# Sample weights, depthwise sums and a leaky ReLU operand of VectorE in PSUM, and query scaling in four pieces

## The chip, the cores and the metric

The kernel runs on one core of one Trainium2 chip. The metric is the device time of one execution in microseconds (us), lower is better. Its engines are named as the profile names them: PE is TensorE, DVE is VectorE, ACT is ScalarE, POOL is GpSimd, SP is SyncE.

## What is computed

The reference adds four layers to an image x of shape (4, 256, 64, 64), each on the group-normalised x. Cut to what the change touches:

```python
# layer 0: deformable convolution, then a gated MLP
y = leaky_relu(bn1(conv1x1(gn(x))), 0.01)
t = leaky_relu(bn(depthwise3x3(y) + dw_b), 0.01)
offset, mask = linear(t), softmax(linear(t), 9 taps)      # G = 4 groups, 9 taps each
samp = bilinear(inproj(y), grid(offset))                   # 4 corners of each tap are read
dout = outproj((samp * mask).sum(taps))
x2   = bn2(y + dout); x3 = x2 * se(x2.mean())
x    = x + y + fc2(leaky_relu(fc1(x3), 0.01))
# layer 1: 3x3 grouped convolution with rotated kernels, modulated
# layer 2: linear attention: q = softmax(q, over the 64 of a head) / 8, k = softmax(k, over pixels)
#          out = Wout . (context(k, v) . q), then batch norm over all images
# layer 3: three grouped convolutions with 4-bit weights
```

## The kernel before, in words

The work is written as programs of the five engines that wait on each other by semaphores. A list called `plan` runs stages for each of the 4 images (b = 0 to 3): A (convolution, depthwise convolution, offsets and masks), F (outproj and MLP), L1, L2, and last L3 for all images. Inside, stage A has loops A1 and A2, F has F1 and F2, L2 has L2a and L2b. Each loop has four turns of two chunks of 512 pixels.

The sampling runs beside these stages, as a stream. POOL does nothing else: for each image it walks over 32 tiles of 128 pixels, and in each over 4 groups. For one tile and one group (a **unit**) it issues 9 indirect DMAs, called gathers here, from the table in HBM into the group's slot of `ring` (L371). So the stream has 4 x 128 = 512 units and 4608 gathers. The slot's semaphore `ring_free` holds POOL back until DVE has used what lies in the slot; with four slots POOL can be four units ahead.

The DVE part of a unit is `unit` in the vector program. It waits for the gathers, multiplies the slot's 2304 numbers a partition with 36 sample weights, each broadcast over 64 channels, in `PARTS` = 4 instructions of 576 numbers (L1340), and sums them with one reduction (L1346). Both `ring` and the weights `wt` are in SBUF. `Stream.give` puts these units between the DVE instructions of the stages. `TURNS` says how many tiles a turn of a stage takes; `extra` puts single tiles (one of 4 units) between stages. That gives these numbers of tiles, over all images:

| where | tiles | units |
|---|---|---|
| A1 / A2 | 12 / 12 | 48 / 48 |
| extra tiles in A, in L1 | 8, 3 | 32, 12 |
| F1 (with the last one) / F2 | 16 / 24 | 64 / 96 |
| L1 / L2a / L2b | 20 / 24 / 9 | 80 / 96 / 36 |

Image 0 passes stage A before the stream begins, and image 3 passes F2, L1, L2 and then L3 runs after it has ended.

Other names that the change touches:

- A2: `depthwise` makes half of the depthwise convolution on DVE: for each of 9 taps and two chunks one instruction on 512 numbers, a product first (L1484), then product and sum (L1486), from `padded` in `img2` into `dwacc`, a piece of `img1` in SBUF. ACT reads `dwacc` and writes `ych`. The other half is on PE, in banks 0 and 2 of the PSUM tensor `PS`.
- F2: for each chunk four quarters q of the hidden layer. PE fills two banks (`up`, semaphore gH), ACT adds the bias into SBUF (gZ), DVE makes the leaky ReLU of 1024 numbers with `leaky` (L1405, both inputs are the same SBUF tile; gB), and PE multiplies the result (`down`, gD). `room(pe, "gZ", ...)` lets PE write a bank again.
- L2a: for each chunk DVE scales `QS`, the exponentials of 512 pixels' queries, 2048 numbers a partition, with the reciprocals `qsum` (L1775), for PE to transpose (cQn).
- `PS` has 8 banks of 512 numbers. A1, F1, F2 and L2a use banks 6 and 7 for their matmuls.

Of the kernel before, what the change touches and what calls it, by code (L numbers as in the profile page):

```python
# [20 lines left out]
ALU = mybir.AluOpType  # L21
# [111 lines left out]
def network_kernel(nc, x, par, wa, wr, wf, wq, w3, out):  # L133
    ctx = ExitStack()
    with ctx:
# [36 lines left out]
        ostats = sb("ostats", [P, KC * B * CHUNKS * 6])  # L172
        sm = sb("sm", [P, 496])
        PS = ctx.enter_context(nc.psum_tensor("PS", [P, 8, 512], F32))

        def v(name, k=None, rows=P):
# [16 lines left out]
        rsums = small(KC * CHUNKS)  # L193
        fb = small(8)
        a_hid, m_hid, ang, sin_c, cos_c, mod = small(1), small(1), small(2), small(2), small(2), small(2)
# [10 lines left out]
        obn4 = small(2 * SETS)  # L206
        assert used[0] <= 496, used[0]

# [5 lines left out]

        dwacc = [img1[:, TILES * 3 * PTS + h * CHUNK:TILES * 3 * PTS + (h + 1) * CHUNK] for h in range(2)]

# [61 lines left out]
        def room(eng, name, n):  # L278
            eng.wait_ge(sem(name), n + 1)
# [28 lines left out]
        for k in range(1, B):  # L308
# [5 lines left out]
                 "L1 last": 1}  # L314

        class Stream:


            def __init__(self, unit, turned=None):
                self.unit, self.turned, self.taken, self.left = unit, turned, {}, []  # L320

            def begin(self, part, gi, i):

                self.left = []
                if gi is not None:
                    n = TURNS[part]
                    self.left = [(gi, i * n + (self.taken.get(gi, 0) + j), g, j) for j in range(n) for g in range(G)]
                self.share = len(self.left)
# [9 lines left out]

            def ended(self, part, gi, turns=PAIRS):
                if gi is not None:  # L340
                    self.taken[gi] = self.taken.get(gi, 0) + TURNS[part] * turns
# [345 lines left out]
        def _(pe):  # L687
# [10 lines left out]
            def group_average():  # L698

                count["gn"] += 1  # L700
                pe.wait_ge(sem("gn_moments"), count["gn"])
                mm(PS[:, 7, 0:4], v("gavg"), ms, True, True).then_inc(sem("gn_grouped"), 1)

# [74 lines left out]
            def F(b):  # L778
# [42 lines left out]
                def f2(i):  # L821
                    for h in range(2):
                        n, c = i * 2 + (b * CHUNKS + h), i * 2 + h

                        def up(q):
                            room(pe, "gZ", n * 4 + q)
                            for j in range(2):
                                for k in range(KC):
                                    at = k * 4 * C + (2 * q + j) * P
                                    last = mm(PS[:, 2 * (q % 2) + j, :], fc1[:, at:at + P], chunk_of(img1, k, c),  # L830
                                              k == 0, k == KC - 1)
                            last.then_inc(sem("gH"), 1)
# [223 lines left out]
        def _(act):  # L1056
# [78 lines left out]
            def F(b):  # L1135
# [20 lines left out]
                def f2(i):  # L1156
                    for h in range(2):
                        n = i * 2 + (b * CHUNKS + h)
                        for q in range(4):
                            done(act, "gH", n * 4 + q)  # L1160
                            room(act, "gB", n * 4 + q)
                            for j in range(2):
                                last = A_(i2[4 + q % 2][:, j * CHUNK:(j + 1) * CHUNK], PS[:, 2 * (q % 2) + j, :], ACT.Identity,
                                          bias=fb[:, 2 * q + j:2 * q + j + 1])
                            last.then_inc(sem("gZ"), 1)
# [156 lines left out]
        def _(dve):  # L1322
# [10 lines left out]
            def unit(b, t, g, j):  # L1333

                dve.wait_ge(sem(f"gathered{g}"), t * (16 * K2) + 16 * K2 * (b * TILES + 1))
                n = K2 * CORNERS // PARTS
                for part in range(PARTS):
                    rg = ring[:, g, part * n * GC:(part + 1) * n * GC].rearrange("p (k c) -> p k c", c=GC)
                    weights = seg(wt, t * (PTS * CORNERS) + (g * PARTS + part) * n, n)
                    last = vec.tensor_tensor(rg, rg, weights.unsqueeze(2).to_broadcast([P, n, GC]), ALU.mult)  # L1340
# [32 lines left out]
            def moments_from(stats_):  # L1373
# [11 lines left out]
                dve.wait_ge(sem("gn_grouped"), q)  # L1385
                link(vec.tensor_copy(gm, PS[:, 7, 0:4]))
                link(vec.tensor_tensor(gsq[:, 0:2], gm[:, 0:2], gm[:, 0:2], ALU.mult))
# [194 lines left out]
            def F(b, gi):  # L1582
# [34 lines left out]
                dve.wait_ge(sem("fc1_shift"), b + 1)  # L1617
                vec.tensor_tensor(fb, PS[:, 5, 0:FC], v("fc1_b"), ALU.add)
                for k in range(KC):
# [5 lines left out]
                def f2(i):  # L1625
                    for h in range(2):
                        n, m, c = i * 2 + (b * CHUNKS + h), i + b * PAIRS, i * 2 + h
                        for q in range(4):
                            done(dve, "gZ", n * 4 + q)
                            room(dve, "gD", n * 4 + q)  # L1630
                            leaky(i2[6 + q % 2], i2[4 + q % 2]).then_inc(sem("gB"), 1)
                            stream.give(1, 8)
# [101 lines left out]
            def L2(b, gi):  # L1734
# [23 lines left out]
                def la(i, last_pair=False):  # L1758
                    for h in range(2):
# [14 lines left out]
                        link(vec.reciprocal(qsum, qsum))  # L1774
                        vec.tensor_tensor(qs3, qs3, qsum.unsqueeze(2).to_broadcast([P, 32, DH]), ALU.mult).then_inc(sem("cQn"), 1)  # L1775
                        done(dve, "cKs", n * 4 + 3)
# [270 lines left out]
```

## Time and profile before

| | us |
|---|---|
| median of 3 runs | 7383.66 |
| lowest, highest | 7372.89, 7388.69 |
| the profiled execution: its own time | 7394.4 |
| its span in the trace | 7392.6 |
| POOL's first gather begins, last ends | 188.9, 6365.7 |

A page of the profile gives for each engine its busy time and share of the span. Groups of instructions have a line of the kernel, engine, operation, out<-in, shapes and count, then busy us, mean ns of one, and the idle time before them with what ended it. The rows of a timeline have start and duration in us, and in brackets the idle time before and its end. "issue" is time in which the profile shows nothing that is waited for.

### The profile page before, as it was taken

Reading aid. Unit: us, or ns where it says so; the run is one execution under the profiler, and the core shown is the slowest. Engines: PE = TensorE matmul, PEld = TensorE weight load, DVE = VectorE, ACT = ScalarE, POOL = GpSimd, SP = SyncE. Lnnn points to the kernel's source line nnn. Section 1 sums busy time; section 2 is a strip of 40 time slices with the busy share of each in tenths; the row PEclk is TensorE's granted clock in tenths of the full one; section 3 lists DMA queues with packets and bytes.
Section 4 is the critical chain, followed back from the end, with each engine's and each line's share of the span. In section 5 each row is a group of like instructions: output and inputs, shape, how many; then the busy total and the mean of one; then the engine's idle time right before and its main releaser. Section 6 shows DMA issues by size and latency. Waiting matters only on the chain.

```text
span 7392.6 us, 45558 instructions
## 1 busy us (share of the span) xinstructions
PE 3808.3 (52%) x10560; PEld 2000.5 (27%) x10560; DVE 5174.9 (70%) x5212; ACT 1073.1 (15%) x1619; POOL 4743.2 (64%) x4676
## 2 busy tenths in 40 slices
PE   7142241341574516533764346426656652497968
PEld 4121120220221204311322124213223431243533
DVE  5778787786777668856777679767777976432546
ACT  2110000100111002211100022111101210111334
POOL 0777777777777777777777777777777777300000
PEclk9576675675787758766887678767878876698979
DMA  3453543634433333364433333554333345310047
GB/s 104 146 149 99 184 133 113 201 111 153 137 123 124 102 103 114 123 221 159 128 118 114 104 112 123 186 181 136 123 113 106 123 152 190 99 37 34 34 168 185
DMA packets 547458, 954.04 MB, mean 129 GB/s; under 512 B 284448, under 2 KB 349984, under 8 KB 531616
## 3 DMA queue, kind: packets, MB, share of 16 engines
q0 software_dynamic: 221184, 604.27, 26.2%
q1 hardware_dynamic: 326176, 348.65, 14.6%
q8 instruction: 38, 0.62, 0.0%
q14 instruction: 60, 0.49, 0.0%
HBM read 792.21 MB, written 160.37 MB: 129 GB/s over the span
## 4 chain that ended last, share of the span: by engine, by line
POOL 50%; issue 22%; PE 12%; DVE 9%; DMA 3%; ACT 1%; SPq 1%; DVEq 0%; POOLq 0%; ACTq 0%
POOL ring L371 50%; PE PS L692 11%; DVE ring L1340 3%; DVE dbuf L1346 2%; DMA img<-d_dram 2%; ACT img L1061 1%; DMA ring<-table,idx_stage 1%; DVE sm L1750 0%; DVE stats L1860 0%; POOL idx_stage L387 0%; SPq L593 0%; DMA img<-q_dram 0%; PE PS L789 0%; DMA o_dram<-img 0%; ACT wb_sb L1061 0%
## 5 line engine op out<-in xcount | busy, mean ns | idle before, releaser
L371 POOL DMA_INDIRECT ring<-table,idx_stage x4608 | 4714.6, 1023 | 1434.9 <-issue 1371.4
L1340 DVE TENSOR_TENSOR ring<-ring,wt 128x576 f32<-128x576 f32 x2048 | 1414.2, 753 | 992.8 <-DMA ring<-table,idx_stage 868.5
L1346 DVE TENSOR_REDUCE dbuf<-ring 128x64 f32<-128x2304 f32 x512 | 2070.2, 4043 | 31.4 <-DMA d_dram<-dbuf 3.3
L692 PE MATMUL PS<-img,wb_sb 128*128 128x512 f32 (+1 forms) x3328 | 1635.2, 652 | 471.0 <-DVE img L1405 299.6
L692 PE MATMUL PS<-img,wa_sb 128*128 (+1 forms) x1984 | 930.1, 630 | 620.9 <-DVE img L1724 244.9
L692 PEld LDWEIGHTS PS<-img,wb_sb 128*128 128x128 f32 x3328 | 689.5, 211 | 1382.7 <-issue 1088.9
L692 PEld LDWEIGHTS PS<-img,wa_sb 128*128 128x128 f32 x1984 | 396.9, 202 | 1124.6 <-issue 1064.5
L692 PE MATMUL PS<-sm,params 128*128 128x4 f32 (+1 forms) x32 | 9.1, 354 | 825.5 <-DVE sm L1384 761.0
L692 PE MATMUL PS<-wa_sb,cb 128*128 128x108 f32 (+1 forms) x1024 | 237.0, 397 | 370.9 <-DVE cb L1405 370.9
L789 PE MATMUL PS<-params,img 128*128 128x128 f32 x256 | 62.9, 426 | 691.2 <-DMA img<-d_dram 691.2
L1061 ACT ACTIVATE img<-PS,sm 128x512 f32<-128x512 f32 x384 | 247.8, 680 | 1090.1 <-PE PS L692 1090.1
L692 PEld LDWEIGHTS PS<-wa_sb,cb 128*128 128x128 f32 x1024 | 212.8, 274 | 413.9 <-DVE cb L1405 386.3
L692 PE MATMUL PS<-cb,img 128*128 128x256 f32 x1024 | 267.0, 413 | 90.0 <-ACT img L1061 90.0
L1061 ACT ACTIVATE img<-PS 128x512 f32<-128x512 f32 (+1 forms) x224 | 173.9, 777 | 726.6 <-PE PS L789 378.5
L1061 ACT ACTIVATE img<-img (+4 forms) x206 | 164.6, 801 | 723.8 <-DVE img L1592 259.3
L970 PE MATMUL PS<-params,img 128*128 128x128 f32 x512 | 108.3, 392 | 300.7 <-ACT img L1061 259.5
L1405 DVE SCALAR_TENSOR_TENSOR img<-img 128x1024 f32<-128x1024 f32 x128 | 155.7, 1217 | 141.9 <-ACT img L1061 141.9
L1061 ACT ACT_TABLE_LOAD x21 | 26.9, 1283 | 1521.9 <-DVE sm L1389 1512.6
L789 PEld LDWEIGHTS PS<-params,img 128*128 128x128 f32 x256 | 50.2, 223 | 710.1 <-issue 681.4
L692 PE MATMUL PS<-wb_sb,img 128*128 128x512 f32 x512 | 233.9, 611 | 12.2 <-ACT img L1061 12.0
L692 PEld LDWEIGHTS PS<-cb,img 128*128 128x128 f32 x1024 | 202.4, 206 | 130.5 <-ACT img L1061 103.8
L692 PEld LDWEIGHTS PS<-sm,params 128*128 128x128 f32 x32 | 8.0, 310 | 834.7 <-issue 513.2
(194 smaller groups left out, 2973.4 us busy)
## 6 DMA issues: line engine op xcount, KB each, us to landing
ring<-table,idx_stage POOLq DMA_INDIRECT x4608
table<-cb SPq DMA_DIRECT2D x64, 512.0 KB, 6.0
img<-y_dram SPq DMA_DIRECT2D x64, 512.0 KB, 6.5
q_dram<-img SPq DMA_DIRECT2D x32, 1024.0 KB, 4.2
img<-q_dram SPq DMA_DIRECT2D x32, 1024.0 KB, 6.2
img<-in_x SPq DMA_DIRECT2D x8, 2048.0 KB, 12.2
y_dram<-cb SPq DMA_DIRECT2D x64, 256.0 KB, 2.3
d_dram<-dbuf SPq DMA_DIRECT2D x128, 128.0 KB
```

The costliest lines, as they stand in the source:

```text
L371: nc.gpsimd.indirect_dma_start(out=ring[:, g, p * CORNERS * GC:(p + 1) * CORNERS * GC], out_offset=None, in_=tab[b], in_offset=bass.Indire ...
L692: return nc.tensor.matmul(o, l, r, start=start, stop=stop, **kw)
L789: last = nc.tensor.transpose(PS[:, 2 * h + k, s * P:(s + 1) * P], i2[h][:, s * C + k * P:s * C + (k + 1) * P], v("ident"))
L970: last = nc.tensor.transpose(PS[:, m, s * P:(s + 1) * P], QS[:, s * HID + m * P:s * HID + (m + 1) * P], v("ident"))
L1061: return nc.scalar.activation(o, i, f, **kw)
L1340: last = vec.tensor_tensor(rg, rg, weights.unsqueeze(2).to_broadcast([P, n, GC]), ALU.mult)
L1346: vec.tensor_reduce(dbuf[:, j, g * GC:(g + 1) * GC], ring[:, g, :].rearrange("p (k c) -> p c k", c=GC), AX_X, ALU.add).then_inc(sem("ring_ ...
L1405: return vec.scalar_tensor_tensor(out=o, in0=i, scalar=SLOPE, in1=i, op0=ALU.mult, op1=ALU.max)
```

## The change

- `wps` is a view of 144 numbers in bank 7 of PSUM. In the stages A2, L1, L1 last and L2b, and in extra tiles (`stream.apart`), DVE copies a tile's weights from `wt` to `wps` before the tile's first unit, waits for that copy, and multiplies the whole slot with one instruction of 2304 numbers. In A1, F1, F2 and L2a the unit stays as it was. Of 512 units 208 are in the first form.
- `dwacc` are banks 1 and 3 of PSUM.
- F2: ACT makes 0.01 x (value + bias), with a second vector `fb_low`; DVE makes max(value + bias, that) in two instructions of 512 numbers that read PSUM themselves. PE gets its banks back from DVE (gB) and no longer from ACT (gZ).
- L2a: the scaling of `QS` is made in four instructions of 512 numbers.
- The average of the group norm moves from bank 7 to bank 6.

```diff
...
+        wps = PS[:, 7, 0:PTS * CORNERS]
...
-        fb = small(8)
+        fb, fb_low = small(8), small(8)
...
         ych = [cb[:, h * 1024:(h + 1) * 1024] for h in range(2)]
         xpt = [cb[:, (2 + h) * 1024:(3 + h) * 1024] for h in range(2)]
-        dwacc = [img1[:, TILES * 3 * PTS + h * CHUNK:TILES * 3 * PTS + (h + 1) * CHUNK] for h in range(2)]
+        dwacc = [PS[:, 2 * h + 1, :] for h in range(2)]
         i2 = [img2[:, j * 1024:(j + 1) * 1024] for j in range(9)]
...
                  "L1 last": 1}
+        APART = ("A2", "L1", "L1 last", "L2b")
+
         class Stream:
             def __init__(self, unit, turned=None):
                 self.unit, self.turned, self.taken, self.left = unit, turned, {}, []
+                self.apart = True
             def begin(self, part, gi, i):
                 self.left = []
+                self.apart = part in APART
                 if gi is not None:
                     n = TURNS[part]
                     self.left = [(gi, i * n + (self.taken.get(gi, 0) + j), g, j) for j in range(n) for g in range(G)]
...
                     self.unit(*self.left.pop(0))
             def ended(self, part, gi, turns=PAIRS):
+                self.apart = True
                 if gi is not None:
                     self.taken[gi] = self.taken.get(gi, 0) + TURNS[part] * turns
...
-                mm(PS[:, 7, 0:4], v("gavg"), ms, True, True).then_inc(sem("gn_grouped"), 1)
+                mm(PS[:, 6, 0:4], v("gavg"), ms, True, True).then_inc(sem("gn_grouped"), 1)
...
                         n, c = i * 2 + (b * CHUNKS + h), i * 2 + h
                         def up(q):
-                            room(pe, "gZ", n * 4 + q)
+                            room(pe, "gB", n * 4 + q)
                             for j in range(2):
                                 for k in range(KC):
                                     at = k * 4 * C + (2 * q + j) * P
...
                             room(act, "gB", n * 4 + q)
                             for j in range(2):
                                 last = A_(i2[4 + q % 2][:, j * CHUNK:(j + 1) * CHUNK], PS[:, 2 * (q % 2) + j, :], ACT.Identity,
-                                          bias=fb[:, 2 * q + j:2 * q + j + 1])
+                                          bias=fb_low[:, 2 * q + j:2 * q + j + 1], scale=SLOPE)
                             last.then_inc(sem("gZ"), 1)
                 loop(ACT.Identity, f2)
                 barrier()
...
             def unit(b, t, g, j):
+                if g == 0:
+                    if stream.apart:
+                        vec.tensor_copy(wps, seg(wt, t * (PTS * CORNERS), PTS * CORNERS)).then_inc(sem("wt_moved"), 1)
+                        dve.wait_ge(sem("wt_moved"), t + (b * TILES + 1))
+                    else:
+                        dve.sem_inc(sem("wt_moved"), 1)
                 dve.wait_ge(sem(f"gathered{g}"), t * (16 * K2) + 16 * K2 * (b * TILES + 1))
-                n = K2 * CORNERS // PARTS
-                for part in range(PARTS):
+                parts = 1 if stream.apart else PARTS
+                n = K2 * CORNERS // parts
+                for part in range(parts):
                     rg = ring[:, g, part * n * GC:(part + 1) * n * GC].rearrange("p (k c) -> p k c", c=GC)
-                    weights = seg(wt, t * (PTS * CORNERS) + (g * PARTS + part) * n, n)
+                    weights = wps[:, g * n:(g + 1) * n] if stream.apart \
+                        else seg(wt, t * (PTS * CORNERS) + (g * PARTS + part) * n, n)
                     last = vec.tensor_tensor(rg, rg, weights.unsqueeze(2).to_broadcast([P, n, GC]), ALU.mult)
                 last.then_inc(sem("weighted"), 1)
                 dve.wait_ge(sem("weighted"), t * G + (b * TILES * G + g + 1))
...
-                link(vec.tensor_copy(gm, PS[:, 7, 0:4]))
+                link(vec.tensor_copy(gm, PS[:, 6, 0:4]))
...
                 vec.tensor_tensor(s_ga, s_g, bninv[:, 4:6], ALU.mult)
                 vec.tensor_tensor(s_gc, s_g, bnsh[:, 4:6], ALU.mult).then_inc(sem("se_gate"), 1)
                 dve.wait_ge(sem("fc1_shift"), b + 1)
-                vec.tensor_tensor(fb, PS[:, 5, 0:FC], v("fc1_b"), ALU.add)
+                link(vec.tensor_tensor(fb, PS[:, 5, 0:FC], v("fc1_b"), ALU.add))
+                vec.tensor_scalar(fb_low, fb, SLOPE, None, ALU.mult)
                 for k in range(KC):
                     w_ = wb_sb[:, F_FC1 + k * 4 * C:F_FC1 + (k + 1) * 4 * C]
                     last = vec.tensor_scalar(w_, w_, s_ga[:, k:k + 1], None, ALU.mult)
...
                         for q in range(4):
                             done(dve, "gZ", n * 4 + q)
                             room(dve, "gD", n * 4 + q)
-                            leaky(i2[6 + q % 2], i2[4 + q % 2]).then_inc(sem("gB"), 1)
+                            for j in range(2):
+                                half = slice(j * CHUNK, (j + 1) * CHUNK)
+                                last = vec.scalar_tensor_tensor(out=i2[6 + q % 2][:, half], in0=PS[:, 2 * (q % 2) + j, :],
+                                                                scalar=fb[:, 2 * q + j:2 * q + j + 1],
+                                                                in1=i2[4 + q % 2][:, half], op0=ALU.add, op1=ALU.max)
+                            last.then_inc(sem("gB"), 1)
                             stream.give(1, 8)
                         done(dve, "gD", n * 4 + 3)
                         dve.wait_ge(sem(f"gYl{h}"), m * 16 + 16)
...
                         qs3 = QS.rearrange("p (a d) -> p a d", d=DH)
                         link(vec.tensor_reduce(qsum, qs3, AX_X, ALU.add))
                         link(vec.reciprocal(qsum, qsum))
-                        vec.tensor_tensor(qs3, qs3, qsum.unsqueeze(2).to_broadcast([P, 32, DH]), ALU.mult).then_inc(sem("cQn"), 1)
+                        for s in range(SUBS):
+                            part = slice(s * HEADS, (s + 1) * HEADS)
+                            last = vec.tensor_tensor(qs3[:, part], qs3[:, part],
+                                                     qsum[:, part].unsqueeze(2).to_broadcast([P, HEADS, DH]), ALU.mult)
+                        last.then_inc(sem("cQn"), 1)
                         done(dve, "cKs", n * 4 + 3)
                         link(vec.tensor_tensor(ksum, ksum, kalpha, ALU.mult))
                         vec.tensor_tensor(ksum, ksum, esum, ALU.add)
```

How the instructions of DVE stand, at three places. First, a unit in the loop of A2, right after the leaky ReLU of `cb` (the names `ych`). Before:

```order
L1405 SCALAR_TENSOR_TENSOR cb<-cb 128x1024
L1335 ISA
L1340 ISA
L1340 TENSOR_TENSOR ring<-ring,wt 128x576
L1340 ISA
L1340 TENSOR_TENSOR ring<-ring,wt 128x576
L1340 ISA
L1340 TENSOR_TENSOR ring<-ring,wt 128x576
L1340 ISA
L1340 TENSOR_TENSOR ring<-ring,wt 128x576
L1342 ISA
L1345 ISA
```

And in the changed kernel, with the reduction that follows in both:

```order
L1420 SCALAR_TENSOR_TENSOR cb<-cb 128x1024
L1344 ISA
L1344 COPY PS<-wt 128x144
L1345 REGISTER_ALU
L1348 REGISTER_ALU
L1355 TENSOR_TENSOR ring<-ring,PS 128x2304
L1357 ISA
L1360 ISA
L1361 TENSOR_REDUCE dbuf<-ring 128x64
```

Four products from two SBUF inputs have become one from SBUF and PSUM, with a copy ahead of the first of a tile's four units.

Second, in F2 the instruction ahead of a unit. Before:

```order
L1358 ISA
L279 REGISTER_ALU
L1405 SCALAR_TENSOR_TENSOR img<-img 128x1024
L1335 ISA
L1340 ISA
L1340 TENSOR_TENSOR ring<-ring,wt 128x576
```

In the changed kernel:

```order
L278 ISA
L281 REGISTER_ALU
L1649 SCALAR_TENSOR_TENSOR img<-PS,sm,img 128x512 x2
L1348 ISA
L1355 ISA
L1355 TENSOR_TENSOR ring<-ring,wt 128x576
```

The leaky ReLU is now two instructions, with one input in PSUM; the unit behind it is as it was.

Third, the query scaling in L2a (`QS` is a part of `img`). Before:

```order
L1773 TENSOR_REDUCE sm<-img 128x32
L127 REGISTER_ALU
L1774 RECIPROCAL sm<-sm 128x32
L127 REGISTER_ALU
L1775 TENSOR_TENSOR img<-img,sm 128x2048
L276 ISA
```

In the changed kernel:

```order
L1794 TENSOR_REDUCE sm<-img 128x32
L127 REGISTER_ALU
L1795 RECIPROCAL sm<-sm 128x32
L127 REGISTER_ALU
L1798 TENSOR_TENSOR img<-img,sm 128x512 x4
L278 ISA
```

One product of 2048 numbers has become four of 512, in the same place. The order on PE is the same in both kernels.

## Rows read from the trace of the kernel before

**Rows 1.** The page: busy time of the engines; the chain that ended last.

```profile
PE 3808.3 (52%) x10560; PEld 2000.5 (27%) x10560; DVE 5174.9 (70%) x5212; ACT 1073.1 (15%) x1619; POOL 4743.2 (64%) x4676
...
POOL 50%; issue 22%; PE 12%; DVE 9%; DMA 3%; ACT 1%; SPq 1%; DVEq 0%; POOLq 0%; ACTq 0%
```

**Rows 2.** Stretches (PE, PEld, DVE, ACT, POOL, clock, DMA, GB/s): image 0's stream, tail.

```profile
189.00:1748.00 1559.00, 493.93 (x1422) 299.53 (x1422) 1226.61 (x1128) 147.31 (x189) 1209.45 (x1169) 0.65 0.46 140
...
6366.00:7393.00 1027.00, 828.83 (x2628) 416.65 (x2628) 441.63 (x661) 286.87 (x356) 0.00 (x0) 0.89 0.29 88
```

**Rows 3.** Gathers: their group on the page; the line's min/median/max ns.

```profile
L371 POOL DMA_INDIRECT ring<-table,idx_stage x4608 | 4714.6, 1023 | 1434.9 <-issue 1371.4
...
L371 POOL DMA_INDIRECT ring<-table,idx_stage x4608: 942/946/4534, 188.9 to 6364.8; - x192
```

**Rows 4.** Timeline of a unit in L1.

```profile
2457.09 2.76 DVE L1340 TENSOR_TENSOR ring<-ring,wt 128x576 f32<-128x576 f32 x4 [4.68 <-DMA ring<-table,idx_stage]
2458.06 1.27 POOL L371 DMA_INDIRECT ring<-table,idx_stage  x1 [0.30 <-issue]
2459.64 1.03 POOL L371 DMA_INDIRECT ring<-table,idx_stage  x1 [0.30 <-issue]
2459.89 4.00 DVE L1346 TENSOR_REDUCE dbuf<-ring 128x64 f32<-128x2304 f32 x1
2460.98 0.95 POOL L371 DMA_INDIRECT ring<-table,idx_stage  x1 [0.30 <-issue]
```

**Rows 5.** Timeline around a query scaling in L2a.

```profile
2993.52 2.29 DVE L1775 TENSOR_TENSOR img<-img,sm 128x2048 f32<-128x2048 f32 x1
2993.94 1.96 POOL L387 COPY idx_stage<-idx 128x72 uint32 x1
...
2996.04 1.65 DVE L1780 SCALAR_TENSOR_TENSOR wb_sb<-wb_sb,sm,PS 128x256 f32<-128x256 f32 x4
...
2997.35 0.94 POOL L371 DMA_INDIRECT ring<-table,idx_stage  x1 [0.30 <-issue]
```

**Rows 6.** Timeline, first in A2 (depthwise), then in F2 (leaky ReLU).

```profile
495.37 5.10 DVE L1486 SCALAR_TENSOR_TENSOR img<-img,params 128x512 f32<-128x512 f32 x7
...
498.68 1.15 POOL L371 DMA_INDIRECT ring<-table,idx_stage  x1 [0.30 <-issue]
...
2090.87 1.22 DVE L1405 SCALAR_TENSOR_TENSOR img<-img 128x1024 f32<-128x1024 f32 x1
2091.79 1.11 POOL L371 DMA_INDIRECT ring<-table,idx_stage  x1 [0.30 <-issue]
```

**Rows 7.** POOL's groups: A2 (477:676.2), F2 (2045:2381.6), L1 (2429:2761), L2a (2761:3139, two rows).

```profile
L371 POOL DMA_INDIRECT ring<-table,idx_stage x144 | 155.4, 1079 | 43.6 <-issue 43.3 <-POOL idx_stage L387 0.3
...
L371 POOL DMA_INDIRECT ring<-table,idx_stage x253 | 260.2, 1029 | 76.7 <-issue 75.6 <-DVE dbuf L1346 0.6 <-POOL idx_stage L387 0.5
...
L371 POOL DMA_INDIRECT ring<-table,idx_stage x254 | 254.2, 1001 | 77.0 <-issue 76.5 <-POOL idx_stage L387 0.5
...
L371 POOL DMA_INDIRECT ring<-table,idx_stage x280 | 288.7, 1031 | 87.5 <-issue 82.9 <-DVE dbuf L1346 4.1 <-POOL idx_stage L387 0.5
L387 POOL COPY idx_stage<-idx 128x72 uint32 x4 | 4.5, 1124 | 0.0
```

**Rows 8.** DVE's groups by shape: a difference with PSUM, the first taps.

```profile
L1768 DVE TENSOR_TENSOR img<-PS,sm 128x1024 f32<-128x1024 f32 x64 | 78.4, 1225 | 2.2
...
L1484 DVE TENSOR_SCALAR img<-img,params 128x512 f32 x24 | 10.5, 478 | 0.0
```

**Rows 9.** DVE's waits: first in A2 (477:663), then in L2a (2812:3140).

```profile
DVE ring L1340 <- DMA ring<-table,idx_stage: 14.6, 5, 3.9
...
DVE ring L1340 <- DMA ring<-table,idx_stage: 18.3, 7, 2.9
```

**Rows 10.** Timeline of the last F2, after the stream: PE, and DVE's wait in it.

```profile
6451.81 53.38 PE L692 MATMUL PS<-img,wb_sb 128*128 x124
...
6459.50 1.23 DVE L1405 SCALAR_TENSOR_TENSOR img<-img 128x1024 f32<-128x1024 f32 x1 [2.21 <-ACT img L1061]
```

More of the change, by code:

```diff
@@ L172, in network_kernel @@
         ostats = sb("ostats", [P, KC * B * CHUNKS * 6])
-        sm = sb("sm", [P, 496])
+        sm = sb("sm", [P, 504])
         PS = ctx.enter_context(nc.psum_tensor("PS", [P, 8, 512], F32))
+        wps = PS[:, 7, 0:PTS * CORNERS]
         def v(name, k=None, rows=P):
@@ L206, in network_kernel @@
         obn4 = small(2 * SETS)
-        assert used[0] <= 496, used[0]
+        assert used[0] <= 504, used[0]
         coef = cb[:, 0:KC * K2 * K2]
```

## The prediction

> **What bounds the kernel now.** The page comes first. DVE has the most busy time, 70%, but the chain that ended last runs through POOL for 50% and through "issue" for 22% of the span [rows 1]. So a stretch view is next: over image 0 POOL is busy 1209 of 1559 us, and after the last gather it does nothing for the 1027 us of the tail [rows 2]. Then the gathers themselves. Their median is 946 ns, the shortest 942, the mean 1023, and 1371 us of the idle time ahead of them is "issue" [rows 3], 0.30 us before each [rows 4]. A gather with nothing in its way therefore costs 0.945 + 0.305 = 1.25 us of POOL, and 4608 of them 5760 us. The stream lasted from 188.9 to 6365.7, 6177 us. The missing 417 us are what can be won in it: 4608 x (1.023 - 0.945) = 360 us in gathers that took longer, the rest in gaps. POOL waited for something that the profile names in 1434.9 - 1371.4 = 63 us at most [rows 3], for DVE 0.6 and 4.1 us in two stages [rows 7].
>
> Why some gathers take longer is seen in a timeline. In L1, while DVE multiplies (2457.09 to 2459.85), one takes 1.27 and one 1.03 us; under the reduction they take 0.95 [rows 4]. I went through all gathers this way: the moment 0.13 us after a gather's start decides. If a DVE instruction with two SBUF inputs is running then, the gather ends 0.815 us after that instruction. This held for 988 of the 1018 gathers that met a product L1340, for 96 of 96 that met L1486, for 91 of 93 that met the leaky ReLU of F2. L1775 held a copy of POOL for 1.96 us, where the copy takes 0.25 alone [rows 5]. Reductions delayed 7 of 1510, and instructions with one tensor input in PSUM none: 0 of 30 for L1780 (SBUF first, PSUM second), 0 of 48 for L1768, 0 of 24 to 29 for L1592, L1636 and L1724. L1780 ran beside a gather of 0.94 us [rows 5].
>
> **A page against the rows.** The Trainium skill (SBUF - State Buffer, "Who interferes with whom") says that a DVE instruction with two SBUF inputs stands in the way of a GpSimd instruction that reads SBUF, and that one with at most one SBUF input does not; the rows agree. But the same section infers that descriptor generation needs the write interface, which tensor_tensor leaves free, so that such a DMA isn't held up. By that the change would be worth nothing, where the sum below gives 180 us. The gather of 1.27 us under a product [rows 4] speaks against it.
>
> **The parts of the change.**
>
> Products, 208 units. The 988 delays under L1340 sum to 216 us with those whose product was the last to end, 0.42 a unit over 512 units; in the stages that change form they are 13 us in the extra tiles of A, 20 in A2, 5 and 37 in L1, 18 in L2b: 93 us, 0.45 a unit. A check from a row: in L1 254 gathers x (1.001 - 0.945) [rows 7] is 14.2 us for 28 units, 0.50, of which some is the kernel rotation ahead of it. All 93 us go, since the new product has one SBUF input, as L1780.
>
> Its own length: before, four take 2.76 us [rows 4]. L1768 has 1024 numbers with PSUM in 1.225 us [rows 8]; scaled up, 2304 give 2.76 us at most, and with one fixed part in place of four about 2.55. The dear end is the rate of the reduction, 4.00 us [rows 4]. I take 2.55, because L1768 is the same kind of instruction. The copy of 144 numbers lies between the 0.16 us of the smallest instructions and the 0.41 of L1780's 256 numbers [rows 5]; 52 of them are 8 to 21 us of DVE, mostly taken back by 208 x 0.2 us. It comes ahead of the wait for gathers, which covers it: 14.6 us of such waits in one A2 [rows 9].
>
> Depthwise sums. 96 gathers met L1486, 0.278 us late each: 27 us over three A2; one takes 1.15 us [rows 6]. A check: in A2 144 gathers x (1.079 - 0.945) [rows 7] is 19.3 us; 16 units take 6.6, the leaky ReLU of `ych` (it stays) 4.6, the rest is 8. All of it goes. The instructions (seven in 5.10 us) should stay near 0.75 us; if the operand and the store in PSUM cost extra, I bound it by 0.1 us: L1780 takes 0.41 us for 256 numbers [rows 5], where a quarter of a leaky ReLU's 1.22 us [rows 6] is 0.31. The first tap may lose a fast form: 0.478 us [rows 8] up to 0.75. That is 8 x 0.27 = 2 us in the first A2, ahead of the stream, where DVE sets the turn; with the other bound 64 x 0.1 = 6 us more. I take 2, since L1768 with PSUM and L1405 without it take the same 1.22 us for 1024 numbers [rows 6, 8].
>
> Leaky ReLU of F2. 91 gathers were held by it for 40 us in the three F2 beside the stream (one, 1.11 us, in [rows 6]); all goes. DVE gets 1.41 us (two L1636) for 1.22, 0.2 us x 32 in an F2. ACT has as much as before. PE's later permission (gB for gZ) costs nothing: `down(q)` stands ahead of `up(q + 2)` and waits for the same gB. In the last F2, with no stream, PE is busy without a gap for 53.38 us while DVE waits 2.21 us for ACT [rows 10], so the 0.2 us are hidden; without that cover they were 6 us.
>
> Query scaling. 24 beside the stream cost 23.5 us in gathers and 11 in index copies (four took 4.5 us instead of 1.0 in one L2a [rows 7]): 35 us, 1.45 each. In four pieces a read waits at most for one piece, some 0.3 us on average, and two reads meet the 2.5 us: 0.6 x 24 = 14 us stay, 20 are won (bounds 10 and 28). DVE pays 0.2 to 0.5 us a chunk. In L2a it has 18.3 us of waits for gathers in 328 [rows 9] against 4 us; at the loop's start, where DVE is four units behind, that may cost POOL 1 us. In the tail the next instruction waits for PE for 0.6 us anyway.
>
> Sum: 93 + 27 + 40 + 20 = 180 us won, 2 + 1 lost: 177. The moves to bank 6 cost nothing. The profiled execution took 7394.4 us, so 7217; the median of the runs is 10.7 below that execution, so **7206 us**.
>
> **Rivals.**
>
> *DVE becomes the bound in A2.* One A2 lasts 186 us with 14.6 of waits for gathers [rows 9], so DVE needs 171.4; POOL loses 20 x 47/62 = 16 us of delay and needs 170. They meet. For it speaks that a dearer tap (0.1 x 64 = 6 us) or product (1.3 x 16 = 21 us) falls on DVE at once; against it, that a slot is refilled up to 30 us after it is free, so that some microseconds are carried to the next stage. Price: 3 x 5 to 3 x 21 us, so 7220 to 7270. Chance 14%.
>
> *More comes back*: 200 to 225 us, if delays that I put down to instructions that stay were partly set off by a product just before them (the 1.79 us gather under a leaky ReLU of `ych` in A2). 7160 to 7185, 10%.
>
> *No gain*: the page's rule, or a delay that the freed time runs into elsewhere: 7375 to 7390, 3%.
>
> *Slower*: the new product still holds POOL's read, although one input is in PSUM. It would do so for 2.5 us in one piece. A query scaling of 2.29 us costs 1.45 us, so this one 1.6, against 0.45 now: 208 x 1.15 = 239 us, less 20 for the scaling in pieces, near 7600. It decides from 0.87 us a unit (0.45 + 87/208, since the other parts gain 87 at most). Against it stand the 30 gathers under L1780. 3%.
>
> **How the numbers follow.** The forecast has 70%, with 7188 to 7228 of its own: 93 +- 8, 27 +- 3, 40 +- 5, the scaling 10 to 28, the head 0 to 6. The range takes in most of the first rival and half of the second: 7178 to 7258. 0.2%, 15 us, is what a measurement of this kernel can tell. Faster 95% (70 + 14 + 10 and a part of the third), within it 2%, slower 3%.
>
> **What would show it.** Right: in the trace after, the mean gather in L1 and L2b falls to about 950 ns, in A2 from 1079 to near 980, in F2 from 1029 to near 985, in A1 it stays near 1017; the whole mean is near 985 and the stream lasts some 6000 us. The product is near 2.55 us. Index copies of 2 us in L2a are gone. The tail stays at 1027 us within 5. Wrong: gathers of 2 to 3 us under the new product (slower); `ring_free` waits of POOL in A2 and no DVE wait for gathers there (DVE is the bound); a first A2 longer by more than 6 us.

## The result, and the profile after

| median, us | before | after | ratio, 95% interval |
|---|---|---|---|
| 4 runs of each | 7382.7 (7372.89 to 7388.69) | 7215.0 (7213.73 to 7224.52) | 0.9776 [0.976, 0.9791] |

The change takes 168 us away, 2.2%. The profiled execution of the changed kernel took 7214.56 us with a span of 7212.8; that of before took 7394.4 with 7392.6. So the spans differ by 179.8 us, where the working had 177.

First the page of the changed kernel (engines and chain, as in [rows 1]), then its gathers as in [rows 3] and the two forms of the product:

```profile
PE 3788.9 (53%) x10560; PEld 1992.8 (28%) x10560; DVE 5180.5 (72%) x4868; ACT 1071.3 (15%) x1619; POOL 4557.7 (63%) x4676
...
POOL 43%; issue 22%; DVE 14%; PE 13%; DMA 4%; ACT 2%; SPq 1%; DVEq 1%; POOLq 0%; ACTq 0%
...
L378 POOL DMA_INDIRECT ring<-table,idx_stage x4608 | 4539.8, 985 | 1439.1 <-issue 1365.4
...
L1355 DVE TENSOR_TENSOR ring<-ring,wt 128x576 f32<-128x576 f32 x1216 | 838.9, 751 | 431.8 <-DMA ring<-table,idx_stage 321.0
L1355 DVE TENSOR_TENSOR ring<-ring,PS 128x2304 f32<-128x2304 f32 x208 | 530.5, 2551 | 368.0 <-DMA ring<-table,idx_stage 364.3
```

POOL is busy 186 us less (4743.2 before, 4557.7 now), 175 of it in the gathers: the same 4608 have a mean of 985 ns, which was 1023. DVE's busy time is the same within 6 us. What is left in the chain is divided differently, since POOL and DVE are now closer, but "issue" with POOL still leads.

The stretches of head, stream and tail (columns as in [rows 2]):

```profile
0.00:189.60 189.60, 141.81 (x474) 88.10 (x474) 112.56 (x173) 40.72 (x57) 0.44 (x5) 0.95 0.36 101
189.60:6185.30 5995.70, 2817.55 (x7458) 1488.21 (x7458) 4618.07 (x3977) 743.87 (x1207) 4557.28 (x4671) 0.72 0.44 141
6185.30:7212.80 1027.50, 829.50 (x2628) 416.47 (x2628) 449.84 (x720) 286.70 (x356) 0.00 (x0) 0.89 0.29 88
```

The head is 0.7 us longer, the stream 181 us shorter (6176.8 before), the tail 0.6 us longer. All of the gain is in the stream.

POOL's groups by stage, to be laid beside [rows 7]: A2 (472:656.4), F2 (1980:2305.9), L1 (2354:2669.6), L2a (2669.6:3040.5, two rows) and L2b (3052.5:3188.1).

```profile
L378 POOL DMA_INDIRECT ring<-table,idx_stage x144 | 140.3, 974 | 43.6 <-issue 42.9 <-POOL idx_stage L394 0.3 <-DVE dbuf L1361 0.3
...
L378 POOL DMA_INDIRECT ring<-table,idx_stage x252 | 249.1, 989 | 76.3 <-issue 75.5 <-POOL idx_stage L394 0.5 <-DVE dbuf L1361 0.3
...
L378 POOL DMA_INDIRECT ring<-table,idx_stage x252 | 238.4, 946 | 76.3 <-issue 75.9 <-POOL idx_stage L394 0.5
...
L378 POOL DMA_INDIRECT ring<-table,idx_stage x279 | 281.9, 1011 | 87.9 <-issue 82.0 <-DVE dbuf L1361 5.3 <-POOL idx_stage L394 0.7
L394 POOL COPY idx_stage<-idx 128x72 uint32 x4 | 1.1, 279 | 0.0
...
L378 POOL DMA_INDIRECT ring<-table,idx_stage x108 | 102.7, 951 | 32.8 <-issue 32.6 <-POOL idx_stage L394 0.2
```

In L1 the mean was 1001 and is 946, which is the duration of a gather with nothing in its way. The reason is in the timeline of a unit in L1 (beside [rows 4]):

```profile
2367.86 0.30 DVE L1344 COPY PS<-wt 128x144 f32 x1
2368.05 0.95 POOL L378 DMA_INDIRECT ring<-table,idx_stage  x1 [0.30 <-issue]
2368.28 2.55 DVE L1355 TENSOR_TENSOR ring<-ring,PS 128x2304 f32<-128x2304 f32 x1
2369.31 0.95 POOL L378 DMA_INDIRECT ring<-table,idx_stage  x1 [0.30 <-issue]
2370.56 0.95 POOL L378 DMA_INDIRECT ring<-table,idx_stage  x1 [0.30 <-issue]
2370.97 4.10 DVE L1361 TENSOR_REDUCE dbuf<-ring 128x64 f32<-128x2304 f32 x1
```

Two gathers start while the product of 2.55 us runs, and neither is late. I went through all gathers of this trace (a gather "meets" the instruction that runs 0.13 us after its start): of some 410 that met a product with its weights in PSUM none was late. Of some 600 that met a product with both inputs in SBUF all but about 20 were, by 0.21 us in the mean. None of some 110 was late under L1501, none of 96 under L1649. The same in A2 under the depthwise taps, in the timeline at 494:

```profile
493.46 2.20 DVE L1501 SCALAR_TENSOR_TENSOR PS<-img,params,PS 128x512 f32<-128x512 f32 x3
494.00 0.95 POOL L378 DMA_INDIRECT ring<-table,idx_stage  x1 [0.30 <-issue]
495.25 0.95 POOL L378 DMA_INDIRECT ring<-table,idx_stage  x1 [0.30 <-issue]
```

What the new instructions cost DVE, by shape:

```profile
L1501 DVE SCALAR_TENSOR_TENSOR PS<-img,params,PS 128x512 f32<-128x512 f32 x256 | 180.7, 751 | 12.5 <-DVE PS L1499 1.9
L1649 DVE SCALAR_TENSOR_TENSOR img<-PS,sm,img 128x512 f32<-128x512 f32 x256 | 179.3, 741 | 138.9 <-ACT img L1068 138.9
L1798 DVE TENSOR_TENSOR img<-img,sm 128x512 f32<-128x512 f32 x128 | 80.7, 690 | 1.1
L1499 DVE TENSOR_SCALAR PS<-img,params 128x512 f32 x24 | 16.8, 745 | 0.0
L1344 DVE COPY PS<-wt 128x144 f32 x38 | 11.5, 301 | 15.8 <-ACTq L302 15.8
```

A tap takes 0.751 us, no more than in SBUF; the first taps went from 478 to 745 ns [rows 8]. The Trainium skill (VectorE: DVE Perf Modes, "Why PSUM operands drop a tier") says that a PSUM operand shuts the mode that spends both SBUF ports on one tensor, and these first taps agree, though of their operands it is the output that moved.

The time that POOL loses in gathers and index copies over 1.25 and 0.25 us and in waits for `ring_free`, put down to what was running or waited for (where several instructions held one gather, to the last), in sums over all images:

| stage | before | after | what moved |
|---|---|---|---|
| A1 | 26.8 | 26.3 | |
| extra tiles in A, in L1 | 29.9, 5.6 | 17.1, 0 | products 13.4 and 5.6 to 0 |
| A2 | 62.4 | 11.7 | products 19.7 to 0, depthwise 26.7 to 0, leaky of `ych` 13.8 to 9.9 |
| F1, with the last one | 59.7 | 59.8 | |
| F2 | 75.7 | 43.5 | leaky 39.7 to 0, products 32.8 to 40.3 |
| L1 | 48.0 | 10.6 | products 37 to 0 |
| L2a | 89.2 | 64.8 | scaling 23.5 to 6.9, copies and waits 20.6 to 11.5 |
| L2b | 20.5 | 2.4 | products 18.1 to 0 |

The differences add up to 182 us, against 181 of the stream. One gather shows what this way of counting does: in the second A2 of the trace before, at 1078.7 us, it took 4.53 us, held by a leaky ReLU of `ych` (0.9 us by itself) and then by the four products behind it, and all of its 3.59 us stand with the products.

### The profile page after: what moved, and what is told of

It is laid out like the page before. It is cut to its first block, busy times and chain, and to the rows that moved or that the text cites. A ratio compares the mean times of both kernels' runs of the same rounds, so it can differ in the third digit from the quotient of the medians.

```text
span 7212.8 us, 44764 instructions
## 1 busy us (share of the span) xinstructions
PE 3788.9 (53%) x10560; PEld 1992.8 (28%) x10560; DVE 5180.5 (72%) x4868; ACT 1071.3 (15%) x1619; POOL 4557.7 (63%) x4676
## 4 chain that ended last, share of the span: by engine, by line
POOL 43%; issue 22%; DVE 14%; PE 13%; DMA 4%; ACT 2%; SPq 1%; DVEq 1%; POOLq 0%; ACTq 0%
POOL ring L378 43%; PE PS L699 12%; DVE ring L1355 5%; DVE dbuf L1361 3%; DMA img<-d_dram 2%; DMA ring<-table,idx_stage 1%; ACT img L1068 1%; DVE sm L1771 1%; DVE sm L1794 0%; DVE sm L1787 0%; DVE stats L1885 0%; DVE img L1798 0%; PE PS L796 0%; DMA img<-q_dram 0%; DVE wb_sb L1805 0%
## 5 line engine op out<-in xcount | busy, mean ns | idle before, releaser
L378 POOL DMA_INDIRECT ring<-table,idx_stage x4608 | 4539.8, 985 | 1439.1 <-issue 1365.4
L1355 DVE TENSOR_TENSOR ring<-ring,wt 128x576 f32<-128x576 f32 x1216 | 838.9, 751 | 431.8 <-DMA ring<-table,idx_stage 321.0
L1355 DVE TENSOR_TENSOR ring<-ring,PS 128x2304 f32<-128x2304 f32 x208 | 530.5, 2551 | 368.0 <-DMA ring<-table,idx_stage 364.3
L1649 DVE SCALAR_TENSOR_TENSOR img<-PS,sm,img 128x512 f32<-128x512 f32 x256 | 179.3, 741 | 138.9 <-ACT img L1068 138.9
```

The lines of the kernel that those rows point to most:

```text
L378: nc.gpsimd.indirect_dma_start(out=ring[:, g, p * CORNERS * GC:(p + 1) * CORNERS * GC], out_offset=None, in_=tab[b], in_offset=bass.Indire ...
L1649: last = vec.scalar_tensor_tensor(out=i2[6 + q % 2][:, half], in0=PS[:, 2 * (q % 2) + j, :], scalar=fb[:, 2 * q + j:2 * q + j + 1], in1=i2 ...
```

## The experiments

The chips on which they ran differ. On two (e9, e10, e11) the kernel before takes 7390 to 7401 us, as in the result; on the three others (e1 to e8, e12) it takes 8584 to 8739. A ratio is always against the kernel before on the same chip. What is different on those chips comes under e1.

**Products alone: e1, e5, e11.** The changed kernel, with the three other parts taken back:

```diff
-        dwacc = [PS[:, 2 * h + 1, :] for h in range(2)]
+        dwacc = [img1[:, TILES * 3 * PTS + h * CHUNK:TILES * 3 * PTS + (h + 1) * CHUNK] for h in range(2)]
...
-                            room(pe, "gB", n * 4 + q)
+                            room(pe, "gZ", n * 4 + q)
...
-                                          bias=fb_low[:, 2 * q + j:2 * q + j + 1], scale=SLOPE)
+                                          bias=fb[:, 2 * q + j:2 * q + j + 1])
...
+                            leaky(i2[6 + q % 2], i2[4 + q % 2]).then_inc(sem("gB"), 1)
...
+                        vec.tensor_tensor(qs3, qs3, qsum.unsqueeze(2).to_broadcast([P, 32, DH]), ALU.mult).then_inc(sem("cQn"), 1)
```

> Only the products of the sampling move to PSUM (208 units); depthwise sums, the leaky ReLU of F2 and the query scaling are as before. Theory (a DVE instruction with two SBUF inputs holds POOL's read until it ends): 93 us less than before, near 7290 us, and mean gathers near 945 ns in L2b. Rival (the gain is that of the whole, or comes mostly from another part): less than 60 or more than 120 us.

> The products alone again, since in the first four runs the kernel before itself took 8728 us: there DMAs that SP issues were reported landed only when POOL paused, and that hid what POOL gains. Where the kernel before takes 7383 us: theory as in the first run, 93 us less, ratio near 0.987. Rival (the parts overlap): ratio under 0.984 or over 0.992.

> The products alone a third time, on a chip where the kernel before takes 7383 to 7400 us if there is one. Theory: 93 us less than before, ratio 0.987 to 0.988, gathers in L2b and L1 near 945 to 960 ns, those in A2 and F2 late by the depthwise sums and the leaky ReLU as before. Rival (the parts overlap, one frees what the next holds): ratio under 0.984 or over 0.991.

e1 gave 8739.03 us against 8728.07, ratio 1.0019 [0.9996, 1.0042]; e5 8627.06 against 8583.67, 1.0044 [1.0016, 1.0072]. Both missed. Yet the gathers had become short: 996 and 994 ns in the mean. So the saving was there and was lost again. The groups and waits of POOL in e1 say where:

```profile
L378 POOL DMA_INDIRECT ring<-table,idx_stage x4608 | 4591.9, 996 | 2788.8 <-issue 1439.7
...
POOL ring L378 <- DVE dbuf L1361: 1346.8, 130, 49.6
```

POOL stood for 1347 us because its ring was full (61 us in the changed kernel of the result). DVE in turn stood for a DMA that SP had issued (L1484 waits for `t_stored`, the stores of L491; the profile puts the end of the wait down to "remote", to no instruction that it shows). The timeline of e1, first SP's issues, then the end of that wait:

```profile
1009.75 3.19 SPq L483 DMA_DIRECT2D y_dram<-cb  x2
1015.98 4.42 SPq L491 DMA_DIRECT2D table<-cb  x2
...
1033.24 0.95 POOL L378 DMA_INDIRECT ring<-table,idx_stage  x1 [0.30 <-issue]
1038.65 1.23 DVE L1484 TENSOR_TENSOR cb<-PS,params 128x1024 f32<-128x1024 f32 x1 [27.96 <-remote]
1039.65 2.12 ACT L1068 ACTIVATE cb<-PS,sm 128x512 f32<-128x512 f32 x3 [28.78 <-remote]
```

The packets of these stores had moved by 1021, but DVE went on at 1038.65 and ACT a microsecond later, 4.5 us after POOL's last gather had ended (1033.24 + 0.95 = 1034.2) and its ring was full. In e1 DVE waited over 8 us for a DMA 56 times, 1326 us in sum; in the kernel before, on the chip of the result, 7 times and 131 us. 51 of the 56 ended with "remote" while the stream ran: in 38 of them POOL had then been idle for over 1.5 us, mostly for 4 to 6, and in 13 it was issuing or had just stopped. I read from this that on these chips the landing of SP's DMA mostly shows only once POOL pauses, and that this lengthens the stream. It is read from the order of times; no run tests it, and issuing isn't told apart from the gathers' own packets, which moved until 1035.6. Why these chips do it and the others not, no run shows.

e11 ran on a chip like that of the result: 7308.7 us (7305.72 to 7315.27) against 7391.68, ratio 0.9889 [0.9872, 0.9905]. The products alone are worth 83 us, where the prediction had 93. Its gathers:

```profile
L378 POOL DMA_INDIRECT ring<-table,idx_stage x4608 | 4625.1, 1004 | 1437.7 <-issue 1371.2 <-DVE dbuf L1361 54.4 <-POOL idx_stage L394 9.4
```

89.5 us less in the gathers, 3.2 us more waits for the ring: 86 us, as its span (7307.0, by 85.6 less). By the table above, the products themselves won 93 to 95 us in the stages that change form. What came back is in the parts left as they were: the leaky ReLU of `ych` in A2 holds POOL for 18.2 us (13.8 before, or 14.7 with its own 0.9 us of the gather of 4.53 us), and the tail is 3 us longer (1030.0 us after the last gather).

**The other parts alone: e2.** `APART = ()` and `self.apart = False` in the changed kernel, so that every unit has the old form.

> The other half: products as before in every stage (four pieces from SBUF), everything else of the change made. Theory: 27 + 40 + 20 = 87 us less than before, near 7296 us, and with the run of the products alone the two add up to the whole, 168 to 180 us, within 10. Rival (the parts overlap, because a gather that one instruction lets go meets the next): the two together exceed or fall short of the whole by over 25 us.

8752.93 us against 8728.07, 1.0024 [1.0001, 1.0046], on the chip of e1, with gathers of 999 ns. Its time says nothing of the parts, for the reason given under e1; its trace does: none of 114 gathers was late under the taps of L1501, none of 80 under L1649. Their worth comes from e9 and e11: the whole change won 168 to 170 us, the products 83, so the rest is 85 to 87 us.

**One product of 2304 numbers with the weights in SBUF: e3, e6, e12.** The kernel before, and one number:

```diff
-PARTS = 4
+PARTS = 1
```

> The kernel before with one product of 2304 numbers a unit, both inputs in SBUF. Theory: each holds POOL for 2.55 us in one piece, at some 1.6 us a unit (a query scaling of 2.29 us cost 1.45) where four pieces cost 0.42: 512 x 1.18 = 600 us more, near 7980 us, if DVE's waits for gathers leave it. Rival (what the change won came from fewer and larger DVE instructions, not from the place of the weights): no slower than before, 7380 us or less.

> The kernel before with one product of 2304 numbers from SBUF again. In the first such run the mean gather rose from 1023 to 1149 ns, 580 us over 4608 gathers. Where the kernel before takes 7383 us, theory: 580 to 600 us slower, near 7970 us, ratio 1.08. Rival (fewer DVE instructions are what helps): ratio 1.00 or less. Second rival (what sped this form up by 7% where the landings were late holds everywhere): ratio 0.93 to 0.97.

> The kernel before with one product of 2304 numbers from SBUF, on a chip where the kernel before takes 7383 to 7400 us if there is one. In the two earlier traces of it 515 and 529 gathers met the product and ended 1.53 and 1.49 us late, where the four pieces cost 1025 gathers 0.207 us each. Theory: 520 x 1.51 - 212 = 573 us more on POOL, near 7960 us, ratio 1.077. Rival (DVE's waits for gathers take part of it in): 1.03 to 1.06. Rival (fewer DVE instructions help): 1.00 or less.

This is the new product's size and length without its operand in PSUM. The timeline of e12 shows two gathers under it, and its page the group:

```profile
2005.14 2.56 DVE L1340 TENSOR_TENSOR ring<-ring,wt 128x2304 f32<-128x2304 f32 x1
2006.37 2.16 POOL L371 DMA_INDIRECT ring<-table,idx_stage  x1 [0.30 <-issue]
...
2011.65 2.54 DVE L1340 TENSOR_TENSOR ring<-ring,wt 128x2304 f32<-128x2304 f32 x1
2012.59 2.43 POOL L371 DMA_INDIRECT ring<-table,idx_stage  x1 [0.30 <-issue]
...
L371 POOL DMA_INDIRECT ring<-table,idx_stage x4608 | 5294.7, 1149 | 1587.9 <-issue 1396.9
```

Each gather ends some 0.8 us after the product: 2005.14 + 2.56 + 0.82 = 2008.52, and the row has 2006.37 + 2.16 = 2008.53. In e3 515 gathers met such a product and were 1.53 us late each, 788 us; the mean went from 1023 to 1149 ns. The stream took 6886 us in e3, 709 more than that of before on the chip of the result. So the "slower" rival's price was real (1.5 us for each gather met, a little over the 1.45 of a query scaling), and it is the PSUM operand that spares it, not the longer instruction.

The times missed in the other direction: 8120.24, 8107.18 and 8126.96 us, against 8728.07, 8583.67 and 8738.7; ratios 0.9319 [0.9293, 0.9344], 0.944 [0.9416, 0.9464] and 0.9286 [0.9246, 0.9325]. All three ran on chips where SP's landings are seen late. With a POOL that is held 1.5 us at each unit they are late less often: DVE waited over 8 us for a DMA 24 times and 394 us in e12, against 56 and 1326 in e1. That the one brings the other isn't shown. The time on a chip like that of the result was not measured; 7390 us and some 580 to 710 us more is an estimate from the delays and from the stream of e3.

**The PSUM product in four pieces: e4.** The changed kernel, with four products of 576 numbers in both forms:

```diff
-                parts = 1 if stream.apart else PARTS
+                parts = PARTS
...
-                    weights = wps[:, g * n:(g + 1) * n] if stream.apart \
+                    weights = wps[:, (g * PARTS + part) * n:(g * PARTS + part + 1) * n] if stream.apart \
```

> The changed kernel with the product from PSUM in four pieces of 576 numbers, as in SBUF before. Theory: PSUM frees POOL whatever the number of pieces, DVE pays 0.2 us a unit which its waits cover: 7215 us within 6. Rival (the single instruction brought the gain): the 93 us of the products come back, near 7308 us.

Its group of the product:

```profile
L1355 DVE TENSOR_TENSOR ring<-ring,PS 128x576 f32<-128x576 f32 x832 | 570.1, 747 | 119.7 <-DMA ring<-table,idx_stage 108.4 <-issue 5.6 <-DVE PS L1501 0.8
```

Some 380 gathers met one of these pieces and none was late; some 470 met a piece with both inputs in SBUF and were 0.22 us late in the mean. Same pieces, same sizes, one operand elsewhere. Its time, 8801.77 us against 8728.07 (1.0089 [1.0064, 1.0113]), belongs to those chips; whether one piece is better than four for the time stays open.

**Query scaling back in one piece: e8.**

```diff
+                        vec.tensor_tensor(qs3, qs3, qsum.unsqueeze(2).to_broadcast([P, 32, DH]), ALU.mult).then_inc(sem("cQn"), 1)
```

> The changed kernel with the query scaling back in one instruction. Theory: 20 to 28 us more than the changed kernel, near 7240 us, and index copies of 2 us return in L2a. Rival (in L2a DVE is the bound, so that the pieces cost what they free): within 5 us of 7215.

8663.43 us against 8583.67, 1.0086 [1.0059, 1.0114]; gathers 989 ns. For the time it is inconclusive: the same chips, and the scaling alone wasn't tried elsewhere. The trace shows the delays: 24 of 29 gathers that met the one instruction were late, by up to 2.10 us and 35.5 us in sum, where in e7, on the same chip, the scaling in four pieces held 18 of 39, by at most 0.49 us and 4.6 us in sum. The index copies of 2 us that were expected did not return; the longest took 0.82 us.

**The other stages' products in nine pieces: e7, e10.** If a read waits for the piece that is running, shorter pieces should cost it less. `PARTS = 9` in the changed kernel makes pieces of 256 numbers in A1, F1, F2 and L2a.

> The changed kernel with the product in nine pieces of 256 numbers in A1, F1, F2 and L2a, where the weights stay in SBUF (304 units); PSUM units unchanged. Theory: POOL waits for the piece that runs, so the 0.42 us a unit shrink with the piece's length to some 0.2: 304 x 0.22 = 67 us less than the changed kernel, near 7150 us, if DVE's dearer train (0.35 us a unit) stays covered; in L2a it has 2 us a tile to spare and needs 1.4. Rival (DVE is the bound in L2a and A1's turns): 7215 us or more.

> The changed kernel with the SBUF products in nine pieces of 256 numbers again, hoped for on a chip where the kernel before takes 7383 to 7390 us. Theory as before: a gather waits only for the piece that runs, 304 units x 0.22 = 67 us less than the changed kernel's 7215 to 7220, near 7150 us, ratio near 0.968. Rival (DVE, which pays 0.35 us more a unit, is the bound in L2a and A1): 7215 us or more, ratio 0.977 or over.

e7 gave 8795.67 us against 8583.67, 1.0235 [1.0205, 1.0265], on a chip of the other kind. e10 gave 7220.51 (7211.63 to 7227.66) against 7400.64, 0.9756 [0.9739, 0.9774]: the time of e9, the changed kernel itself on the same chip. Of the 67 us that were expected nothing came. The pieces and gathers of e10:

```profile
L1355 DVE TENSOR_TENSOR ring<-ring,wt 128x256 f32<-128x256 f32 x2736 | 943.9, 417 | 337.4 <-DMA ring<-table,idx_stage 228.0 <-DMA wt<-w_dram 81.0 <-DMA wb_sb<-in_wf 23.4
...
L378 POOL DMA_INDIRECT ring<-table,idx_stage x4608 | 4531.8, 983 | 1451.0 <-issue 1368.0 <-DVE dbuf L1361 70.7 <-POOL idx_stage L394 9.6
```

The mean of the some 600 delays fell only from 0.21 to 0.18 us. The timeline shows why:

```profile
1887.30 3.09 DVE L1355 TENSOR_TENSOR ring<-ring,wt 128x256 f32<-128x256 f32 x9
...
1888.41 2.80 POOL L378 DMA_INDIRECT ring<-table,idx_stage  x1 [0.30 <-issue]
...
2054.43 2.77 DVE L1355 TENSOR_TENSOR ring<-ring,wt 128x256 f32<-128x256 f32 x8 [3.43 <-DMA ring<-table,idx_stage]
...
2055.33 1.02 POOL L378 DMA_INDIRECT ring<-table,idx_stage  x1 [0.30 <-issue]
2056.65 1.04 POOL L378 DMA_INDIRECT ring<-table,idx_stage  x1 [0.30 <-issue]
```

Most gathers lose some 0.1 us or less now, as the last two of these rows. But some 25 of the 600 did not get in between two pieces: the one at 1888.41 ends at 1891.21, 0.82 us after the last of nine pieces (1890.39). These few make some 50 us. With four pieces such gathers are rarer: 3 or 4 in the trace before, 3 in e9. So the products' delays fell by some 20 us only (131 in e9, 111 in e10). 11 us of that went into POOL's waits for its ring (70.7 us, 59.4 in e9), for which the train of nine, 3.10 us of DVE instead of 2.75, is the likely cause. "DVE is the bound", the rival, had the time right, but only these 11 us speak for it.

**The changed kernel again: e9**, beside e10 and e11.

> The changed kernel itself, since in the eight runs so far the kernel before took 8584 to 8728 us and no measurement of the changed one stands beside them. Where the kernel before takes 7383 us: 7215 us, ratio 0.977. Where it takes 8600 us or more: if what a part gains on POOL is lost again in DMAs of SP that are reported landed late, the ratio is 1.00 to 1.01, as with the products alone; if the parts still add up, it is under 0.99.

7220.1 us (7212.02 to 7222.39) against 7390.43, 0.9765 [0.9749, 0.9781]. The result holds on a second chip. The changed kernel itself did not run on one of the other three; variants of it (e1 and e5, e2, e4, e8) were 0.2 to 0.9% slower there than the kernel before, and e7 2.4%. That the change gains nothing there is therefore likely, and not measured.

## Why the prediction was right, by its own steps

**What bounds the kernel.** Right. POOL's gathers set the stream, 181 us fell out of POOL's time, and the stream is 181 us shorter.

**The rule of who holds up whom.** Right, and it is the step that all the rest hangs on. An operand in PSUM takes the delay away (0 of some 410 products, 0 of some 110 taps, 0 of 96 leaky ReLUs; e4), the same instruction with both inputs in SBUF gives it 1.5 us a gather (e3, e6, e12). Both rules of the Trainium skill (SBUF - State Buffer, "Who interferes with whom") can now be read against this: the one on a DVE instruction with two SBUF inputs agrees with every number here; the inference that descriptor generation isn't held up by tensor_tensor doesn't hold for these gathers. Of an instruction with at most one SBUF input the prediction gives the rule short: the page exempts it only outside the modes that use both ports, and the traces agree. Three tensor_scalars of 1152 numbers with one tensor input, all in SBUF (L1536, L1539 and L1542 before), held each of the 9 gathers that met them, by 0.12 to 0.22 us. The first taps held 4 of 4 before, and 0 of 13 once they wrote PSUM.

**Products, 93 us.** In the changed kernel they won 13.4 + 19.7 + 5.6 + 37 + 18.1 = 94 us where the form changed. Alone (e11) they brought 83 us in the time. The term was right as the delay that goes; it left out what comes back. A gather that isn't late under one instruction starts sooner and can meet another: the leaky ReLU of `ych` took 4.4 us more in e11 (0.9 of it by the way of counting), the products of F2, still in SBUF, 7.5 us more in the whole change. The product takes 2.551 us, the copy 0.30, between the bounds.

**Depthwise sums, 27 us.** 26.7 measured, and the tap kept its 0.75 us. The first taps took 0.745, as bounded, but of the 2 us that this was to cost in the head only 0.7 are there.

**Leaky ReLU of F2, 40 us.** 39.7 went, but 7.5 came back in the products, so F2 won 32. The mean gather of F2 is 989 ns, where 985 was said.

**Query scaling, 20 us.** Undersized: 16.6 went under the scaling and 9 in the index copies and waits beside it: some 26 with the waits, inside the 10 to 28. The copy that took 2 us is gone; four take 1.1 us now. The 1 us of POOL at the start of L2a is in its 5.3 us of waits for the ring (4.1 before).

**DVE as the bound in A2.** It didn't happen, but it came near. DVE's waits for gathers, first in A2 and then in L2a, stand beside [rows 9]:

```profile
DVE ring L1355 <- DMA ring<-table,idx_stage: 4.5, 2, 2.6
...
DVE ring L1355 <- DMA ring<-table,idx_stage: 10.4, 3, 4.2
```

The first row is of the 144 gathers of an A2 and reaches 12 us past its loop; over the same gathers DVE waited 18.4 us before. In the loop itself (472 to 644) 1.9 us are left of the 14.6. The loop took 172 us, so DVE needed 170, as the prediction had it (171.4), and POOL waited for DVE 1.1 us in the three A2. (The prediction's 20 x 47/62 is 15 and not 16 us, which moves nothing.) A further saving for POOL in A2 would find DVE.

**The sum and the offset.** 177 us were worked out, and the two profiled executions differ by 179.8: 8 less in F2, 6 more in the scaling, 4 more in the leaky ReLU of `ych` and 1 in the head make up the 3 us. The 9 us between 7206 and 7215 are the last step, "the median of the runs is 10.7 below that execution". Before's profiled execution lay 10.7 us above its median and above the highest of its other runs (7388.69); the changed kernel's lies at its median, 7214.56 and 7215.0. I carried the distance over as if it belonged to the kernel. Without that step the sum gives 7217. That this lies within 2 us of 7215 is in part luck: the terms missed by up to 8 us each way and cancelled, and against the medians the sum of 177 us is 9 us too much. Between medians the gain is 168 us, and 170 in e9, so of the 179.8 us some 10 belong to the one execution of before.

## What to carry to other kernels

When an engine that issues DMAs sets the pace, look at its issues one by one and ask what the neighbour runs at each late one: here 6% of the stream hid in such delays, mostly of 0.1 to 1.5 us, that no wait names, and half of it was won. Moving one operand of VectorE to PSUM took them away at no cost in VectorE's time, while cutting the product into nine pieces kept a tail of long delays and cost VectorE more. And try a result on more than one chip: here some chips are bound by something else, and there the parts of this saving brought nothing.

## What the runs showed of the hardware

- On three of the chips used, DMAs that SP issued were mostly taken for landed only after POOL had stopped issuing gathers (38 of 51 long waits in e1): a wait of 28 us where the packets had moved 17 us before its end, 1326 us of such waits in e1. The kernel before takes 8584 to 8739 us there and 7383 to 7401 elsewhere. A kernel whose gathers are each held up longer (e3, e6, e12) is 6 to 7% faster there. Neither was expected, and the cause stays open.
- Under short pieces that follow each other (417 ns, started every 335 ns), 4% of the gathers waited for the end of the whole train, up to 2.3 us (e10). With the pieces of 0.75 us started every 0.667 us, many of the delays were only 0.09 us.
- A multiply-add of 512 numbers with PSUM input and output takes 0.751 us, as in SBUF; a plain multiply with a scalar went from 0.478 to 0.745 us when it wrote PSUM.
